# A fused four-layer block stack on one core: the softmax division of the attention moves from GpSimd to VectorE

## What is computed

```
x = x + L0_attn(norm(x))   # inside it x + attn(norm(x)), then x + MLP (256 -> 1024 -> 256, GELU)
x = x + L0_ffn(norm(x))    # RWKV channel mix: sigmoid(r) * (relu(k)^2 W_v)
x = x + L1_attn(norm(x))   # Mamba: convolution, 512 channels x 16 states, a scan over time
x = x + L1_ffn(norm(x))    # one of 8 experts per sequence, chosen by the mean token
...
# the attention, with 16 heads of 16 channels and a window of 128:
scores = q k^T * scale; scores outside the band -> -inf     # 128 queries x 256 keys
attn   = softmax(scores)                                    # exp(s - max) / sum
out    = attn v
```

## Time and profile before

| | |
|---|---|
| median of three runs | 3138.97 us |
| the profiled execution: its time, its span | 3140.19 us, 3138.4 us |
| mean granted TensorE clock | 0.946 |
| busy: PE, DVE, ACT, POOL | 88%, 80%, 77%, 85% |
| POOL, multiplying by B and C (L1826, L1836) | 1201.6 us and 1145.4 us |
| VectorE, the recurrence (L1599) | 586.1 us and 590.1 us |

### The profile page before, as it was taken

The page is one execution under the profiler, slowest core; times in us unless marked ns, Lnnn a source line. Parts: engine busy times, 40 slices in busy tenths (PEclk is TensorE's granted clock), DMA queues, the critical chain, the costliest instruction groups (busy, mean ns, idle before and its releaser), DMA issues. The chain is left out here.

```text
span 3138.4 us, 54529 instructions
## 1 busy us (share of the span) xinstructions
PE 2770.5 (88%) x17328; PEld 1768.4 (56%) x17328; DVE 2498.8 (80%) x5626; ACT 2402.0 (77%) x5299; POOL 2657.6 (85%) x1596
## 2 busy tenths in 40 slices
PE   5888887899999999999899999989999998988667
PEld 3554454465665656566565656656565665654336
DVE  3257979888787978888787887978788897889880
ACT  6587879788787978888797887879798787865532
POOL 1108999999999999999999999999999999999880
PEclk9899999999999999999999999999999999998778
DMA  3004353446445454644546364445546455365541
GB/s 85 14 36 151 122 186 121 164 142 219 135 149 174 154 193 134 222 144 145 173 150 204 124 224 141 153 154 157 201 130 222 143 162 172 125 216 163 191 145 42
DMA packets 285965, 477.31 MB, mean 152 GB/s; under 512 B 38450, under 2 KB 93362, under 8 KB 285682
## 3 DMA queue, kind: packets, MB, share of 16 engines
q1 hardware_dynamic: 285682, 473.83, 46.0%
HBM read 388.79 MB, written 84.93 MB: 151 GB/s over the span
## 5 line engine op out<-in xcount | busy, mean ns | idle before, releaser
L1826 POOL TENSOR_TENSOR h_rows<-u_rows,b_rows 128x1024 f32<-128x1024 f32 x512 | 1201.6, 2370 | 39.3 <-PE bank L968 29.9
L1836 POOL TENSOR_TENSOR h_rows<-h_rows,c_rows 128x1024 f32<-128x1024 f32 x486 | 1145.4, 2369 | 43.6 <-DVE state L1606 30.2
L1280 ACT ACTIVATE bank<-d_rows,a_rep 128x512 f32<-128x512 f32 x1024 | 673.3, 687 | 236.6 <-DMA d_rows<-delta_dram 55.8
L1599 DVE TENSOR_TENSOR_SCAN h_rows<-bank,h_rows 128x512 f32<-128x512 f32 x492 | 586.1, 1211 | 37.0 <-ACT bank L1280 34.2
L1599 DVE TENSOR_TENSOR_SCAN h_rows<-bank,state,h_rows 128x512 f32<-128x512 f32 x480 | 590.1, 1266 | 25.9 <-ACT bank L1280 21.3
L1105 ACT ACTIVATE prob<-prob,neg_max 128x256 f32<-128x256 f32 x1024 | 508.8, 503 | 15.8 <-DVE neg_max L1377 15.6
L1377 DVE CUSTOM_DVE_ANT_0 prob<-bank,bands 128x256 f32<-128x256 f32 x896 | 335.1, 417 | 124.5 <-PE bank L803 84.9
L815 PE MATMUL bank<-ident,prob 128*128 128x128 f32 x2048 | 330.3, 286 | 59.8 <-ACT prob L1105 29.0
L815 PEld LDWEIGHTS bank<-ident,prob 128*128 128x128 f32 x2048 | 241.1, 144 | 223.1 <-issue 148.0
L968 PE MATMUL bank<-h_rows,sum_n 128*32 128x512 f32 x2048 | 297.0, 665 | 62.7 <-POOL h_rows L1836 48.3
L1036 PE MATMUL bank<-y4T,w 128*128 128x256 f32 x1024 | 248.5, 391 | 19.5 <-DMA e_b<-in_b 12.5
(11 more groups left out here) (164 smaller groups left out, 4856.1 us busy)
## 6 DMA issues: line engine op xcount, KB each, us to landing
u_rows<-u_dram SPq DMA_DIRECT2D x256, 256.0 KB, 4.1
d_rows<-delta_dram SPq DMA_DIRECT2D x256, 256.0 KB, 4.1
b_rows<-bc_dram SPq DMA_DIRECT2D x256, 256.0 KB, 3.1
c_rows<-bc_dram SPq DMA_DIRECT2D x256, 256.0 KB, 3.1
w<-in_W SPq DMA_DIRECT2D x28, 1024.0 KB, 7.0
zs_dram<-region_b SPq DMA_DIRECT2D x64, 256.0 KB, 3.3
xc_dram<-region_b SPq DMA_DIRECT2D x64, 256.0 KB, 2.8
u_dram<-region_b SPq DMA_DIRECT2D x64, 256.0 KB, 4.5
```

The source lines that it names most:

```text
L1280: e.activation(banks[at.bank][:, :], d_rows[:, c, :], ACT.Exp, scale=a_rep[:, k:k + 1]).then_inc(filled[at.bank], 1)
L1599: e.tensor_tensor_scan(rows, banks[at.bank][:, :], rows, start, ALU.mult, ALU.add).then_inc(drained[at.bank], 1)
L1826: e.tensor_tensor(half_of(i, b, half), u_rows[:, 2 * half:2 * half + 2, :], twice(b_rows[:, b % 2, :]), ALU.mult).then_inc(bx_ready.sem, 1)
L1836: e.tensor_tensor(rows, rows, twice(c_rows[:, b % 2, :]), ALU.mult).then_inc(hc_ready.sem, 1)
```

## The change

`widen` and `divide` move from GpSimd to VectorE with their steps (`beat`) in the attention unchanged. `divide` now reads the values in the bank and the turned reciprocals in SBUF. ScalarE copies only the 128 columns of turned reciprocals, into `rdenT`, and no longer frees the bank: `divide` does, one step later. TensorE's projection waits for the 8 banks to be free in place of a semaphore of GpSimd's, and so does the load of the next input, which lands in `z`, for the last four of them. ScalarE's expert step drops one wait for weights that TensorE waits for too, and waits for the copy of the last transposed bank, which it does itself, where it waited for that bank's filling. All tables of the order are new; which quads VectorE multiplies is unchanged.

```
 PLACES = {
     "head": (
-        -1814, -1814, -921, 471, 810, 828,
+        -1964, -1421, -619, 484, 484, 758,
...
-                out.append((f"a{n // 4}", ATT0 + 2 * n + 13, ATT0 + 2 * n + 14))
+                out.append((f"a{n // 4}", ATT0 + 2 * n + 13, ATT0 + 2 * n + 15))
...
         def pe_attention(e, i):
...
-            e.wait_ge(*aT_ready.at(i, 8))
+            for w in range(8):
+                e.wait_ge(*gone(use(f"a{w}")))
...
         def act_attention(e, i):
...
-            def copy_values(w):
+            def copy_rden(w):
                 at = use(f"a{w}")
                 e.wait_ge(*full(at))
                 if w > 3:
-                    e.wait_ge(*aT_ready.at(i, w - 3))
-                e.activation(ao[:, w % 4, :, :], banks[at.bank][:, 0:2 * P].rearrange("p (a t) -> p a t", a=2),
-                             ACT.Copy).then_inc(drained[at.bank], 1)
+                    e.wait_ge(*gone(use(f"a{w - 4}")))
+                e.activation(rdenT[:, w % 4, :], banks[at.bank][:, P:2 * P], ACT.Copy).then_inc(rdenT_ready.sem, 1)
...
         def dve_attention(e, i):
...
+            def divide(w):
+                c, k = divmod(w, 2)
+                at = use(f"a{w}")
+                e.wait_ge(*rdenT_ready.at(i, w + 1))
+                e.tensor_tensor(aT[:, k, c * P:(c + 1) * P], banks[at.bank][:, 0:P], rdenT[:, w % 4, :],
+                                ALU.mult).then_inc(drained[at.bank], 1)
...
+            def widen(w):
+                k = w % 2
+                e.wait_ge(*rden_ready.at(i, w + 1))
+                if w > 1:
+                    e.wait_ge(*full(use(f"a{w - 2}")))
+                e.tensor_copy(rden_wide[:, k * P:(k + 1) * P].rearrange("p (h d) -> p h d", d=HD),
+                              rden[:, 8 * k:8 * k + 8].rearrange("p (h o) -> p h o", o=1).broadcast_to([P, 8, HD])
+                              ).then_inc(rden_wide_ready.sem, 1)
...
+                if beat % 8 == 7 and beat >= 15:
+                    divide((beat - 15) // 8)
+                if beat % 8 == 3 and beat >= 11:
+                    widen((beat - 11) // 8)
...
         def pool_attention(e, i):
...
-            def widen(w):
...
-            def divide(w):
...
```

More of the change, by code:

```diff
@@ L103 @@
 THREADS = (
[L104 to L110, removed]
+    (("head", "attention",), (-10939, -4627, -4875, -4872, -4820, -4854, -4850, -4872, -4878, -4883, -4878, -4892, -4877, -4896, -4886, -4947)),
+    (("mlp", "rwkv", "middle",), (-4552, -4876, -4846, -4818, -4843, -4845, -4871, -4853, -4865, -4871, -4876, -4861, -4883, -4883, -4937, -4966)),
+    (("scan",), (-4861, -4844, -4812, -4838, -4840, -4857, -4841, -4861, -4862, -4867, -4850, -4870, -4871, -4916, -4987, -5092)),
+    (("back",), (-4848, -4759, -4855, -4830, -4840, -4811, -4844, -4821, -4840, -4868, -4802, -4900, -5100, -4820, -5710, -4066)),
+    (("route",), (-582, -4952, -6756, -4972, -5815, -4890, -4709, -4907, -5011, -4822, -7182, -4833, -4658, -5273, -2359, -3211)),
+    (("fetch",), (-4916, -5824, -6255, -6497, -4866, -5048, -5344, -4447, -6339, -4943, -5148, -5039, -4306, -2730, -3036, 1212)),
+    (("expert",), (-4808, -4830, -4853, -4848, -4843, -4851, -4918, -4876, -4862, -4860, -4878, -4941, -4998, -7007, 1894, 3458)),
 )
@@ L207 @@
         "head": (
[L208 removed]
+            224, -175, 534, 132, 191, -16,
         ),
         "attention": (
[5 rows of a table removed]
[5 rows of a table added]
         ),
         "mlp": (
[L218 to L219 removed]
+            119, -97, -588, 395, 0, 0, 0, 142, -65, 533, -400, -694, 231, 348, 122, 0, 0, 0, 78, -654, -158, -46,
+            459, -1349, -46, -101, 34, 238, 2, -169,
         ),
         "rwkv": (
[L222 removed]
+            2, 0, -75, 0, 115, -317, -764, 10, -130, 138, -564, 126, 28, -234, -14, 40, -9, 70, -719, -116,
         ),
         "middle": (
[L225 to L226 removed]
+            173, -257, -697, -127, 54, 40, -3, 146, 0, 0, 346, 63, -55, -165, 305, 244, -414, -413, 222, -150, 154,
+            -289, 185, -730, 236, 0, 0, -115, 125,
         ),
         "scan": (
[8 rows of a table removed]
[7 rows of a table added]
         ),
         "back": (
[L239 removed]
+            -237, 0, -63, 0, 0, 0, 126, -8, -8, -311, -8,
         ),
         "route": (
[L242 removed]
+            22, -300, -339,
+        ),
+        "fetch": (
+            54,
         ),
         "expert": (
[L245 to L246 removed]
+            53, 63, 244, -218, -6, -102, -57, -57, -45, -57, -57, -450, -265, -183, 0, 98, 325, 185, 98, -257, 16,
+            -921, -182, -332, -430,
         ),
@@ L1315, in act_expert @@
         def act_expert(e, i):
-            e.wait_ge(*w1_there(i))
-            if i + 1 < 2 * BATCH:
-                e.wait_ge(*full(uses["back", i + 1, "t5.1"]))
             for half in range(2):
@@ L1322, in act_expert @@
                     at = uses["expert", i, f"e{half}.{j}"]
+                    if j == 0 and half == 0 and i + 1 < 2 * BATCH:
+                        e.wait_ge(*gone(uses["back", i + 1, "t5.1"]))
                     e.wait_ge(*full(at))
@@ L1722, in use @@
                 return uses["attention", i, name]
-            def widen(w):
-                k = w % 2
-                e.wait_ge(*rden_ready.at(i, w + 1))
-                if w > 1:
-                    e.wait_ge(*full(use(f"a{w - 2}")))
-                e.tensor_copy(rden_wide[:, k * P:(k + 1) * P].rearrange("p (h d) -> p h d", d=HD),
-                              rden[:, 8 * k:8 * k + 8].rearrange("p (h o) -> p h o", o=1).broadcast_to([P, 8, HD])
-                              ).then_inc(rden_wide_ready.sem, 1)
-            def divide(w):
-                c, k = divmod(w, 2)
-                e.wait_ge(*gone(use(f"a{w}")))
-                e.tensor_tensor(aT[:, k, c * P:(c + 1) * P], ao[:, w % 4, 0, :], ao[:, w % 4, 1, :],
-                                ALU.mult).then_inc(aT_ready.sem, 1)
             yield
@@ L1749, in pool_attention @@
             for beat in range(AFTER - ATT0):
-                if beat % 8 == 3 and beat >= 11:
-                    widen((beat - 11) // 8)
-                if beat % 8 == 7 and beat >= 15:
-                    divide((beat - 15) // 8)
                 yield
@@ L1877, in sp_attention @@
             if i + 1 < 2 * BATCH:
-                e.wait_ge(*aT_ready.at(i, 8))
+                for w in range(4, 8):
+                    e.wait_ge(*gone(uses["attention", i, f"a{w}"]))
                 e.dma_start(x_in[:, :, :], x_view[i + 1]).then_inc(x_landed.sem, 16)
```

127 lines of the change are left out of this document (58 added, 69 removed), and 153 rows, old and new, of tables (LEADS, PLACES).

## The result

The change makes the kernel slower: 3218.78 us, the median of 4 runs (3210.28 to 3225.81), against 3138.80 us for the kernel before in the same comparison. The ratio is 1.0252, with a 95% interval of 1.0234 to 1.0269: 80 us more where 85 us less was forecast.

The account below looks back on a forecast made before the run. GpSimd's work and small waits were taken to bound the kernel, TensorE almost as full. 14 groups x 6.1 us = 85 us less, the freed waits set off against VectorE's stalls: 3054 us, forecast range 3035 to 3085, wider range 3000 to 3125.

Parts of the forecast that it names:

- The period is GpSimd's work and small waits, with TensorE almost as full beside it.: In the middle, per group of 181.95 us: GpSimd busy 169.7, TensorE 169.5, no long wait to remove.
- 14 x 6.1 = 85 us: Gain from GpSimd's side: 6.1 us a group of divide and widen taken off, over 14 groups with a busy GpSimd.
- No change: Rival, whole kernel: TensorE is the real bound, GpSimd only follows, time stays at 3139 us; chance 0.05.
- VectorE's 10.5 us: Work added to VectorE a group: 2.4 us of divide and 8.1 of widen, against 28.3 us free.
- VectorE's stalls go through: Rival on VectorE: its idle time shrinks too little; 3202 us if by 6, 3286 if not at all; chance 0.09.
- the bank that is held one step longer: In the attention, held until divide: counted as nothing under GpSimd's other work, else up to 2.4 us a group.
- the prices of both instructions: On VectorE, 8 of each a group: divide some 0.295 us, widen 1.01 us, bounds 0.2 and 2.28.
- VectorE's work a group: VectorE goes from 153.6 to 164.1 us a group, 157.6 to 174.2 with the two bounds.
- the copy waits for GpSimd while GpSimd loses nothing: In widen on VectorE: the copy waits for GpSimd's running instruction to end; GpSimd's next starts on time.
- The signal named beforehand for a wrong prediction: GpSimd's waits on VectorE's states, recurrence and statistics grow over 4.4 us a group, or TensorE's mask or decay waits replace GpSimd's.
- VectorE's share in the middle: VectorE's busy share in the middle of the run should be near 93%.
- one whole multiplication of GpSimd's, 2.28 us: In widen on VectorE: upper bound on one copy's cost, from the routing instructions' longest times.

Follow-up runs that it names:

- before_pool_light: The kernel before with GpSimd's multiplication by C over only half the columns, the other half of the products left out: 3122.90 us, ratio 0.9936.
- old_widen_reduce: The kernel before with only the widening moved to VectorE, as a reduction over one element; division stays on GpSimd, order of before: 3139.85 us, ratio 1.0000.
- old_widen_long: The kernel before with only the widening moved to VectorE, as a reduction over seven equal elements, long as the copy but never waiting: 3202.07 us, ratio 1.0186.
- old_reduce: The changed kernel with the order tables and ScalarE expert-step waits of before, and the widening as a reduction, not a copy: 3328.14 us, ratio 1.0590.

## Why the prediction was wrong

**The step that failed** is the one that the sum rests on: "The period is GpSimd's work and small waits, with TensorE almost as full beside it." before_pool_light shows that it is not: 34 us a group off GpSimd move the period by 0.3 us. GpSimd follows the others: relieved, it only idles more. The first term, 14 x 6.1 = 85 us, was therefore worth nothing or nearly so: 34 us a group gave 20 us in all. In old_widen_reduce the widening leaves GpSimd, VectorE gets no more than 0.29 us for each, and the time stays. The rival "No change", at a chance of 0.05, had half of this mechanism, that GpSimd only follows; that TensorE is the bound in its place isn't shown.

**The second half of that step**, that VectorE's 10.5 us fit into its 28.3 us of slack, failed as well. The rival "VectorE's stalls go through" gave 3202 us if the idle time shrank by 6 us of 10.5. It shrank by 3.6 of 8.7 and the kernel took 3219. That VectorE's time goes through at six tenths is shown by old_widen_long in the old order; in the new one the copies' 96 us above the reductions cost 46, about half. The windows of the eight stretches show the place: the copies' price stands in the fourth, the sixth and the third, and VectorE is at 97 to 98% in the last two.

**The sum as the runs give it.** The changed kernel is 80 us above the kernel before. 46 of them are the copy's price in the new order (3218.78 less 3172.61). Another 32 are what the division and the new order cost together (3172.61 less 3141.04 in that comparison; the 2 us that are missing lie between the two comparisons); in the old order the division's part alone was 188 us (old_reduce less old_widen_reduce), of which the new tables take back 155.5. The prediction gave the new order no term and put the bank that is held one step longer at nothing, or 2.4 us a group if GpSimd's work did not cover it. That cover was not there, and what the two cost is the third thing that it had wrong.

**What was right:** the prices of both instructions, GpSimd's 163.6 us a group, VectorE's work a group (162.4 against 164.1), and that the copy waits for GpSimd while GpSimd loses nothing: its multiplications take 2363 ns where they took 2367. By the Trainium skill's page "SBUF — State Buffer" (section "SBUF: two separate sides") VectorE's two-port modes take the lock, and its page "Vector Engine (DVE) Microarchitecture Reference" (5.1) lists copies among the instructions of such a mode, and no reductions. The runs agree with both: 199 to 8169 ns for the copy, 257 to 289 for the reduction.

The signal named beforehand for a wrong prediction came too: GpSimd's waits on states, recurrence and statistics grew by over 4.4 us a group. For states and recurrence alone, (45.3 + 36.6 - 16.5 - 8.8) / 10 = 5.7; those for the statistics shrank by 0.7, so 5.0 together. VectorE's share in the middle is 87%, where 93% was named.

**What stays open.** No relief found one engine whose work alone sets the period. TensorE is the nearest to it, at 98.9% in six of eight stretches, but 12.0 us a group off its list gave only 3.4; VectorE, at 94 to 96% in two of the shortened stretches, is the likely next, which is argued, not shown. Why the new order with the reduction is still 1% above the kernel before isn't settled: weights, stores, half of TensorE's products by `w_2`, VectorE's tail and half of GpSimd's product were each taken away, and against the kernel before with the same relief it stayed 0.6 to 2.1% longer each time. TensorE's longer list in the sixth stretch is the nearest candidate; no run took anything off it. No version that computes the whole reference beats the kernel before: the widening alone as a reduction equals it. The new order without the division on VectorE was not tried.

## What to carry to other kernels

In a pipeline of in-order engines, a busy share of 93% doesn't make an engine the bound when another has 93% too: cut one period at events along a group's path and look for the engine that is full in each stretch, and before moving work off an engine, leave out several times as much of it and see whether the time moves at all. Idle time of the receiving engine isn't slack either; price added time by where it stands, with an instruction of the same length that waits for nothing. A widening in SBUF beside a busy GpSimd was much shorter as a reduction over an axis of one element: 0.29 us against 1.04 here.

## What the hardware showed that was not expected

One copy lasted 8.17 us. The forecast took one whole multiplication of GpSimd's, 2.28 us, as its upper bound. The timeline of the kernel after at 889 us, first GpSimd, then VectorE (start, length):

```profile
887.52 4.68 POOL L1837 TENSOR_TENSOR h_rows<-h_rows,c_rows 128x1024 f32<-128x1024 f32 x2
892.15 4.68 POOL L1827 TENSOR_TENSOR h_rows<-u_rows,b_rows 128x1024 f32<-128x1024 f32 x2
896.78 2.34 POOL L1837 TENSOR_TENSOR h_rows<-h_rows,c_rows 128x1024 f32<-128x1024 f32 x1
...
890.81 0.20 DVE L1397 RECIPROCAL rden<-den 128x8 f32<-128x8 f32 x1
891.04 8.17 DVE L1404 COPY rden_wide<-rden 128x128 f32<-128x128 f32 x1
899.13 0.41 DVE L1377 CUSTOM_DVE_ANT_0 prob<-bank,bands 128x256 f32<-128x256 f32 x1
```

The copy starts at 891.04, inside a pair of multiplications that ends at 892.20. It doesn't get its turn there, nor at the end of the next pair's two (896.83), and ends at 899.21 with the last one (899.12), after which GpSimd has a pause. So the wait need not end with the running instruction: where GpSimd's instructions follow each other without a gap, a copy can lose several times in a row. It happened once in 128 copies here: the other 77 that waited got their turn at the first end.
